# Finer pieces in the last turns of a streamed attention

## The reference

```python
def _L0_xattn_ref(query, ref, Wq, bq, Wk, bk, Wv, bv):
    Q = query @ Wq + bq
    K = ref @ Wk + bk
    V = ref @ Wv + bv
    scores = jnp.einsum('bqh,bkh->bqk', Q, K)
    attn = jax.nn.softmax(scores, axis=-1) * norm_fact
    return jnp.einsum('bqk,bkh->bqh', attn, V)

x = x + _L0_xattn_ref(_layernorm(x, axis=-1), ctx_1024, ...)
x = x + _L0_attn_ref(_layernorm(x, axis=-1), ...)
x = x + _L0_ffn_ref(_layernorm(x, axis=-1), ...)
```

## Time and profile before

| | us |
|---|---|
| median of three runs | 237.54 |
| the profiled execution | 237.44 |
| its span | 235.6 |
| TensorE matmul busy | 223.4 (95%) |
| VectorE busy | 138.4 (59%) |
| ScalarE busy | 134.2 (57%) |
| GpSimd busy | 106.0 (45%) |

### The profile page before, as it was taken

One profiled execution on the slowest core, in us unless ns is written; L12 is line 12 of the kernel. 1 busy time (PEld: TensorE's weight loads), 2 busy tenths in 40 slices (PEclk: granted clock), 3 DMA queues, 4 the chain that ended last, 5 costly groups with the idle time before them and its releaser, 6 DMA issues.

```text
span 235.6 us, 4164 instructions
## 1 busy us (share of the span) xinstructions
PE 223.4 (95%) x1537; PEld 190.3 (81%) x1537; DVE 138.4 (59%) x328; ACT 134.2 (57%) x251; POOL 106.0 (45%) x67
## 2 busy tenths in 40 slices
PE   7989999999999989779998999999999999999994
PEld 7747777777777767679987999874689999999993
DVE  3236555555555555625996777516144749977784
ACT  5145666665555557325795576636315858766570
POOL 1065566666666667330599940000000535555450
PEclk9999999999999999999999999999999999999999
DMA  6999999999999991699800000000000585970000
GB/s 207 370 425 415 417 417 420 415 420 418 419 418 418 405 424 78 239 432 420 334 3 3 0 3 0 1 3 0 0 0 3 181 335 200 406 307 3 3 0 22
DMA packets 8531, 52.92 MB, mean 225 GB/s; under 512 B 953, under 2 KB 1218, under 8 KB 6466
## 3 DMA queue, kind: packets, MB, share of 16 engines
q1 hardware_dynamic: 8514, 52.69, 55.8%
HBM read 52.56 MB, written 0.13 MB: 224 GB/s over the span
## 4 chain that ended last, share of the span: by engine, by line
PE 76%; DVE 9%; DMA 6%; ACT 4%; issue 2%; SPq 1%; POOL 1%; ACTq 0%; DVEq 0%; POOLq 0%
PE psum L440 34%; PE psum L508 14%; PE psum L744 8%; PE psum L435 7%; DMA late_sb<-in_ctx_T 6%; PE psum L639 3%; PE psum L626 2%; PE psum L431 2%; PE psum L668 2%; PE psum L695 1%; DVE work L1167 1%; DVE ring L1205 1%; DVE ring L1190 1%; DVE w_lo L1341 1%; POOL ring L387 1%
## 5 line engine op out<-in xcount | busy, mean ns | idle before, releaser
L368 POOL TENSOR_TENSOR ctx_lo<-ring,ctx_hi 128x1792 fp32r<-128x1792 f32 x13 | 52.5, 4035 | 39.8 <-ACT ctx_hi L808 39.8
L423 POOL TENSOR_TENSOR h_lo<-ring,h_hi 128x512 fp32r<-128x512 f32 x16 | 24.8, 1550 | 66.9 <-ACT h_hi L1000 61.0
L440 PE MATMUL psum<-late_sb,work 128*128 128x448 f32 x112 | 44.7, 542 | 1.2 <-DMA late_sb<-in_ctx_T 1.2
L440 PEld LDWEIGHTS psum<-late_sb,work 128*128 128x128 f32 x112 | 20.2, 190 | 18.1 <-issue 17.6
L815 ACT ACTIVATE probsT_hi<-psum 128x512 fp32r<-128x512 f32 (+1 forms) x28 | 13.7, 541 | 31.9 <-PE psum L435 31.9
L1060 DVE TENSOR_REDUCE smalls<-psum 128x1 f32<-128x896 f32 x14 | 15.3, 1092 | 23.1 <-PE psum L440 23.1
L440 PE MATMUL psum<-xT,late_sb 128*128 128x128 f32 x224 | 26.2, 276 | 0.1
L440 PEld LDWEIGHTS psum<-xT,late_sb 128*128 128x128 f32 x224 | 25.5, 192 | 0.3 <-DVE xT L1311 0.3
L808 ACT ACTIVATE ctx_hi<-ring 128x1792 fp32r<-128x1792 f32 x13 | 22.1, 1698 | 2.7 <-DMA ring<-in_ctx 2.7
L508 PE MATMUL psum<-ctx_hi,probsT_hi 128*128 128x256 f32 x98 | 20.6, 326 | 2.5 <-DVE probsT_lo L1084 2.5
L1084 DVE TENSOR_TENSOR probsT_lo<-psum,probsT_hi 128x512 fp32r<-128x512 f32 (+1 forms) x28 | 16.2, 620 | 7.4 <-ACT probsT_hi L815 7.4
(11 more groups left out here) (243 smaller groups left out, 420.3 us busy)
## 6 DMA issues: line engine op xcount, KB each, us to landing
late_sb<-in_ctx_T SPq DMA_DIRECT2D x14, 896.0 KB, 14.0
ring<-in_ctx SPq DMA_DIRECT2D x14, 896.0 KB, 12.8
late_sb<-in_late SPq DMA_DIRECT2D x10, 825.0 KB, 12.5
late_sb<-in_experts SPq DMA_DIRECT2D x8, 1024.0 KB, 6.3
late_slots<-in_experts SPq DMA_DIRECT2D x8, 1024.0 KB, 7.8
early_sb<-in_early SPq DMA_DIRECT2D x1, 512.0 KB, 3.7
early_sb<-in_early SPq DMA_DIRECT2D x1, 465.0 KB, 17.6
work<-in_levels SPq DMA_DIRECT2D x1, 416.0 KB, 20.0
```

The lines of the kernel that those rows point to most:

```text
L368: nc.gpsimd.tensor_tensor(ctxNv[1][:, r % 2], ring[:, r], ctxNv[0][:, r % 2], ALU.subtract).then_inc(s["ctx_lo"], 1)
L423: nc.gpsimd.tensor_tensor(hT[1][:, e % 2, at, :], h32[:, at, :], hT[0][:, e % 2, at, :], ALU.subtract).then_inc(s["h_lo_done"], 1)
L440: last = nc.tensor.matmul(o, lhs(c), rhs(c), start=(c == 0), stop=(c == n - 1))
```

## The change

Four things are done, the first in every turn and the others in the last turns.

1. `attend` takes the terms in the order high x high, high probabilities x low context, low probabilities x high context. It waits for the high probabilities at the start of each part and for the low ones at their first use. It can be called for a stretch of its terms (`first`, `end`) and with another division of the tiles (`cut`).
2. The last group's scores step `scores_ready` after each half. VectorE takes the maximum half by half, and ScalarE the exponential in two halves of 448 with two row sums, each with its own `exp_done`. SP waits for one more `scores_ready`.
3. The last group's probabilities are transposed as three tiles and four, the three ahead of the last three terms of the attend of group 12 and the four behind them. High and low parts and the last attend follow that division. The small exponential for `al` stands between the two high parts, the low context of three tiles ahead of the accumulation of group 12, and the row sums behind the low parts.
4. O is updated, transposed, copied and multiplied by halves of 128 columns, the transposes into banks 0 and 2.

```diff
-            def attend(g, r, last_group=False):
-                pe.wait_ge(s["acc_done"], g + 1)
-                pe.wait_ge(s["ctx_lo"], g + 1)
-                terms = [(t, a, b) for tiles in (range(4), range(4, GT)) for a, b in ((0, 0), (1, 0), (0, 1)) for t in tiles]
-                for i, (t, a, b) in enumerate(terms):
-                    if i == 0:
-                        pe.wait_ge(s["probsT_lo"], g * 2 + 1)
-                    if i == 4 * 3:
-                        pe.wait_ge(s["probsT_lo"], g * 2 + 2)
-                        if last_group:
+            def attend(g, r, first=0, end=3 * GT, cut=4, last_group=False):
+                if first == 0:
+                    pe.wait_ge(s["acc_done"], g + 1)
+                    pe.wait_ge(s["ctx_lo"], g + 1)
+                terms = [(t, a, b) for tiles in (range(cut), range(cut, GT)) for a, b in ((0, 0), (0, 1), (1, 0)) for t in tiles]
+                for i in range(first, end):
+                    t, a, b = terms[i]
+                    q = 0 if t < cut else 1
+                    if t == cut * q and (a, b) == (0, 0):
+                        pe.wait_ge(s["probsT_hi"], g * 2 + q + 1)
+                        if last_group and q == 1:
                             pe.wait_ge(s["last_lo"], 1)
+                    if t == cut * q and a == 1:
+                        pe.wait_ge(s["probsT_lo"], g * 2 + q + 1)
...
+            def last_transposes(q, tiles):
+                pe.wait_ge(s["exp_done"], NG + q)
+                pe.wait_ge(s["probsT_lo"], 2 * (NG - 1))
+                transposes([(bank[4 + q][:, k * P:(k + 1) * P], probs[:, t * P:(t + 1) * P]) for k, t in enumerate(tiles)], s["probs_transposed"])
...
-            scores(NG - 1, (NG - 1) % RING, 16 * ((NG - 1) // RING + 1))
-            attend(NG - 2, (NG - 2) % RING)
-            probs_transposes(NG - 1)
-            attend(NG - 1, (NG - 1) % RING, last_group=True)
+            scores(NG - 1, (NG - 1) % RING, 16 * ((NG - 1) // RING + 1), halves=True)
+            attend(NG - 2, (NG - 2) % RING, end=18)
+            last_transposes(0, range(0, 3))
+            attend(NG - 2, (NG - 2) % RING, first=18)
+            last_transposes(1, range(3, GT))
+            attend(NG - 1, (NG - 1) % RING, cut=3, last_group=True)
...
-            transposes([(half(bank[0], c), half(O, c)) for c in range(DC)], s["o_T"])
-            pe.wait_ge(s["o_copied"], 1)
-            wide(bank[1][:, 0:D], lambda c: half(OT, c), lambda c: wv[:, c, :]).then_inc(s["att_ready"], 1)
+            for c in range(DC):
+                pe.wait_ge(s["acc_done"], NG + 2 + c)
+                nc.tensor.transpose(half(bank[2 * c], 0), half(O, c), ident).then_inc(s["o_T"], 1)
+            for c in range(DC):
+                pe.wait_ge(s["o_copied"], c + 1)
+                last = nc.tensor.matmul(bank[1][:, 0:D], half(OT, c), wv[:, c, :], start=(c == 0), stop=(c == DC - 1))
+            last.then_inc(s["att_ready"], 1)
...
+            for hf in range(2):
+                nc.scalar.activation(probs[:, hf * HALF:(hf + 1) * HALF], bank[2 * b + hf][:, 0:HALF], ACT.Exp, bias=s_("nb", b, b + 1),
+                                     accum_out=s_("rowsum", hf, hf + 1)).then_inc(s["exp_done"], 1)
+            act.wait_ge(s["pv_done"], g)
+            for q, tiles in ((0, range(0, 3)), (1, range(3, GT))):
+                act.wait_ge(s["probs_transposed"], g * 2 + (q + 1))
+                nc.scalar.activation(probsT[0][:, tiles[0]:GT if q else 3, :], bank[4 + q][:, 0:len(tiles) * P].rearrange("p (t q) -> p t q", q=T),
+                                     ACT.Copy).then_inc(s["probsT_hi"], 1)
+                if q == 0:
+                    nc.scalar.activation(s_("al", b, b + 1), s_("M", (r + 1) % RING, (r + 1) % RING + 1), ACT.Exp, scale=-1.0,
+                                         bias=s_("M", r, r + 1)).then_inc(s["alpha_done"], 1)
+            for c in range(DC):
+                act.wait_ge(s["o_T"], c + 1)
+                nc.scalar.activation(half(OT, c), bank[2 * c][:, 0:P], ACT.Copy).then_inc(s["o_copied"], 1)
...
+            for hf in range(2):
+                dve.wait_ge(s["scores_ready"], NG + hf)
+                dve.wait_ge(s["mx_done"], 2 * g + 2 * hf)
+                V.tensor_reduce(s_("mx"), bank[2 * b + hf][:, 0:HALF], AX, ALU.max).then_inc(s["mx_done"], 1)
+                dve.wait_ge(s["mx_done"], 2 * g + 2 * hf + 1)
+                V.tensor_scalar(new, s_("mx"), s_("qb"), s_("M", r, r + 1) if hf == 0 else new, ALU.add, ALU.max).then_inc(s["mx_done"], 1)
+            dve.wait_ge(s["mx_done"], 2 * g + 4)
+            V.tensor_scalar(s_("nb", b, b + 1), new, -1.0, s_("qb"), ALU.mult, ALU.add).then_inc(s["max_ready"], 1)
             dve.wait_ge(s["dve_chain"], chain[0])
             V.tensor_tensor(ctxNv[1][:, g % 2, at], ring[:, g % RING, at], ctxNv[0][:, g % 2, at], ALU.subtract).then_inc(s["last_lo"], 1)
+            accumulate(g - 1, (g - 1) % 2)
...
+            for c in range(DC):
+                V.scalar_tensor_tensor(half(O, c), half(O, c), s_("al", b, b + 1), half(bank[6 + b], c), ALU.mult, ALU.add).then_inc(s["acc_done"], 1)
```

More of the change, by code:

```diff
@@ L333, in _ @@
                 part(i, "late2_in")
-            sp.wait_ge(s["scores_ready"], NG)
+            sp.wait_ge(s["scores_ready"], NG + 1)
             for j in range(SLOTS):
@@ L477, in _, with scores @@
             nc.tensor.matmul(bank[3][:, 0:D], sixteenth[:, :], bv_sb[:, :], start=True, stop=True).then_inc(s["bv_ready"], 1)
-            def scores(g, r, filled, first=False):
+            def scores(g, r, filled, first=False, halves=False):
                 if not first:
@@ L486, in scores @@
                                 lambda c: ringT[:, r, c, hf * HALF:(hf + 1) * HALF])
-                last.then_inc(s["scores_ready"], 1)
+                    if halves or hf == 1:
+                        last.then_inc(s["scores_ready"], 1)
             def probs_transposes(g, first=False):
@@ L495, in probs_transposes @@
                                s["probs_transposed"])
-            def attend(g, r, last_group=False):
-                pe.wait_ge(s["acc_done"], g + 1)
-                pe.wait_ge(s["ctx_lo"], g + 1)
-                terms = [(t, a, b) for tiles in (range(4), range(4, GT)) for a, b in ((0, 0), (1, 0), (0, 1)) for t in tiles]
-                for i, (t, a, b) in enumerate(terms):
-                    if i == 0:
-                        pe.wait_ge(s["probsT_lo"], g * 2 + 1)
-                    if i == 4 * 3:
-                        pe.wait_ge(s["probsT_lo"], g * 2 + 2)
-                        if last_group:
+            def attend(g, r, first=0, end=3 * GT, cut=4, last_group=False):
[9 more added lines that the diff above has]
+                        if last_group and q == 1:
                             pe.wait_ge(s["last_lo"], 1)
+                    if t == cut * q and a == 1:
+                        pe.wait_ge(s["probsT_lo"], g * 2 + q + 1)
                     last = nc.tensor.matmul(bank[6 + r % 2][:, 0:D], probsT[a][:, t, :], ctxNv[b][:, r % 2, t, :],
                                             start=(i == 0), stop=(i == len(terms) - 1))
-                last.then_inc(s["pv_done"], 1)
+                if end == 3 * GT:
+                    last.then_inc(s["pv_done"], 1)
+            def last_transposes(q, tiles):
+                pe.wait_ge(s["exp_done"], NG + q)
+                pe.wait_ge(s["probsT_lo"], 2 * (NG - 1))
+                transposes([(bank[4 + q][:, k * P:(k + 1) * P], probs[:, t * P:(t + 1) * P]) for k, t in enumerate(tiles)], s["probs_transposed"])
             pe.wait_ge(s["g_done"], 1)
@@ L529, in _ @@
             probs_transposes(NG - 2)
-            scores(NG - 1, (NG - 1) % RING, 16 * ((NG - 1) // RING + 1))
-            attend(NG - 2, (NG - 2) % RING)
-            probs_transposes(NG - 1)
-            attend(NG - 1, (NG - 1) % RING, last_group=True)
-            pe.wait_ge(s["tables_in"], 16)
-            pe.wait_ge(s["acc_done"], NG + 2)
-            transposes([(half(bank[0], c), half(O, c)) for c in range(DC)], s["o_T"])
-            pe.wait_ge(s["o_copied"], 1)
-            wide(bank[1][:, 0:D], lambda c: half(OT, c), lambda c: wv[:, c, :]).then_inc(s["att_ready"], 1)
+            scores(NG - 1, (NG - 1) % RING, 16 * ((NG - 1) // RING + 1), halves=True)
[4 more added lines that the diff above has]
+            attend(NG - 1, (NG - 1) % RING, cut=3, last_group=True)
+            pe.wait_ge(s["tables_in"], 16)
+            for c in range(DC):
[5 more added lines that the diff above has]
+            last.then_inc(s["att_ready"], 1)
             keep_warm(11)
@@ L836, in _ @@
             nc.scalar.activation(ctxNv[0][:, g % 2, at], ring[:, g % RING, at], ACT.Copy).then_inc(s["ctx_hi"], 1)
[L837 to L841, removed]
+            b, r = g % 2, g % RING
+            act.wait_ge(s["max_ready"], NG)
+            act.wait_ge(s["probs_transposed"], 2 * g)
+            act.wait_ge(s["acc_done"], NG)
```

(30 more changed lines are left out.)

## The result

| | before | changed |
|---|---|---|
| median of the runs, us | 237.62 (6 runs, 237.04 to 239.20) | 235.89 (6 runs, 235.10 to 236.64) |
| the profiled execution, us | 237.44 | 236.64 |
| its span, us | 235.6 | 234.8 |
| TensorE matmul busy, us | 223.4 | 226.2 |

The ratio is 0.9927, with a 95% interval of 0.9907 to 0.9947: 1.73 us less by the medians. A second set of six runs gave 235.51 us and a ratio of 0.9908 (0.9877 to 0.9940). The forecast was 235.3, or 2.17 us less.

A forecast was written before the change was run, and what follows sets the result against it. TensorE was taken to bound the steady turns, with 3.5 us idle in the last turns. 1.81 us up to the last attend plus 0.36 for O's halves is 2.17: 237.44 - 2.17 = 235.27, said 235.3; range 234.6 to 236.5.

The forecast's parts named there:

- Group 11: Its attend, needing low parts last, starts 0.72 us earlier; 0.35 is kept, as group 12's transposes wait for the exponential.
- The maximum in two halves: Last group: first half reduced before the last scores end, saving 0.49 us; bounds nothing and 0.55; exponential starts at 96.00.
- The exponential: Last group's, in two halves: first transpose loads 0.79 us after its start instead of 1.16, 0.37 less.
- TensorE's order: Transposes placed around group 12's last three terms: ScalarE's high part released at 97.78, last attend at 98.41 instead of 100.22.
- O: After the last attend, update, transposes and copy by halves save 0.36 us of 2.75 before x's update; bounds 0 and 0.6.
- Rest: Expert weights start 0.35 and 1.8 us earlier, no gain put down; everything after the attention stays in the same order.
- rival (d): A fixed event after the attention takes back up to all of the gain: 235.5 to 237.4 us; chance 0.07.
- Rival (b): 28 more waits on TensorE over all 14 attends cost 0.14 us each, 3.9 us: slower, 239.2 us; chance 0.06.
- Rival (a): Pieces cost what they save; only the order of terms gains, 1.07 us: 236.4 us; chance 0.15.
- Rival (c): ScalarE released by the transposes, or group 12's exponential no limit: up to 0.35 us more gain, 234.9 us; chance 0.12.

The follow-up runs named there:

- Experiment 8: Changed kernel with last group's VectorE context copy on ScalarE, ScalarE's last high parts released earlier, and VectorE copying three of group 12's context tiles: median 235.01 us, ratio 0.9885.
- experiment 2: Changed kernel with the last group's maximum and exponential each in one piece again: 236.01 us (one run).
- Experiments 4: Changed kernel with VectorE's copy of three context tiles moved between the two halves of the maximum, while GpSimd's subtraction runs: 237.99 us (one run).
- experiment 5: Changed kernel with VectorE's copy of three context tiles given to ScalarE: median 235.18 us, ratio 0.9896.
- experiment 10: Changed kernel with five more already satisfied waits in every attend, 70 in all on TensorE: median 235.61 us.
- experiment 1: Kernel before with only the new order of terms and the later wait for the low parts, in all attends: median 236.37 us, ratio 0.9931.
- experiment 6: Changed kernel with ScalarE's last high parts released after the 18th term of group 12's attend instead of its last: 235.50 us (one run).

## Why the prediction was right, and where it was off

Sign and mechanism were right, and the time lies in the range. Step by step, with the changed kernel's times less 0.97:

- *Group 11.* Its attend starts at 88.84 - 0.97 = 87.87 (87.88 forecast), released by ScalarE's high part. The transposes of group 12 load at 90.74 (90.74 forecast), held by the exponential. Experiment 8 takes this hold away and brings 0.34 of the 0.37 us that it kept back.
- *The maximum in two halves.* Here the prediction failed. It put the gain at 0.49 us, and its bounds named "nothing (the first half delayed)", but it took the time before the last scores to be enough for the first reduce without working out where VectorE's copy would then lie. Moved up by 0.38 us, the copy started 0.60 us before GpSimd's end instead of 0.22 and was held until then. GpSimd's end had not moved (10.25 us after the common point in both kernels), so the copy's end did not either: 10.66 before, 10.67 changed, which is 95.19. The first reduce started at 95.11, the second at 96.13 and not at 95.74, when the last scores were there (by experiment 2, 94.70 - 83.48 after the common point; in the changed profile itself, the transfer that SP issues on the same step starts at 95.73). The exponential started at 97.34 - 0.97 = 96.37, not 96.00. Against experiment 2, whose exponential starts 96.38 - 83.48 = 12.90 us after the common point, the changed kernel's 97.34 - 84.52 = 12.82 is all that the halved maximum brings: 0.08 and not 0.49. The saving of one reduce was sized well (1.09 less 0.62 = 0.47 us); it was the condition that failed, that the first one is done in time. Experiments 4, 5 and 8 show the copy and GpSimd as the cause.
- *The exponential.* From its start to the first transpose's load 98.12 - 97.34 = 0.78 us (0.79 forecast), as the 0.37 left over in experiment 2 also says (0.45 - 0.08).
- *TensorE's order.* ScalarE's high part was released by the end of group 12's attend, 99.06 - 98.40 = 0.66 us after the last three terms' first load, at 98.09. That is 0.31 after the 97.78 forecast: the 0.37 of the exponential, less some 0.05 since the three transposes took 98.40 - 98.12 = 0.28 and not 0.33. The last attend starts at 99.70 - 0.97 = 98.73, 0.32 after the forecast, and runs 2.78 us to O's update without a wait at its seventh term. The low context of three tiles took 1.02 us and not the 0.84 estimated, and was hidden all the same.
- *O.* 104.88 - 102.48 = 2.40 us, 0.35 less than before (0.36 forecast).
- *Rest.* Nothing came back later, so rival (d) is out. Rival (b) is out by the steady turns and experiment 10. Rival (a) is out too: without the pieces D is 21.08 (experiment 1) and with them 20.36. A pair of pieces does cost more than the whole, 2 x 0.62 against 1.09 us for the reduce, but half of each pair lay off the path, and what was lost was lost to a neighbour on another engine. Rival (c) did not happen: ScalarE was released by the attend's end, and the exponential of group 12 was the limit. Its price was about right, since experiment 6 takes the one away for 0.29 us and experiment 8 the other for 0.34.

So the sum was 2.17, and D shows 1.84. The 0.33 between them is in the main one term, mis-sized: 0.41 too much for the halved maximum. Against it stand 0.04 by which the last scores came earlier than forecast (95.74 - 0.97 = 94.77 against 94.81) and the 0.05 of the transposes; 0.01 was missing at O. That the first profile lay at 236.64 and not near 235.7 is the start's 0.97.

What the Trainium skill says of small tiles ("VectorE: DVE Perf Modes", on the TRN2 errata) is about operations that read SBUF, while the maximum, the exponential and the copies of O read PSUM here; it was a weak support for rival (a). On VectorE's copy of the context the Trainium skill has the matching rule, which I had not drawn on: "SBUF — State Buffer", section "SBUF: two separate sides", says that GpSimd and certain VectorE operations want the same pair of ports, and that whichever starts first has it for its whole instruction while the other waits. By that rule the copy ends a fixed time after GpSimd's instruction, and the rows agree: 0.41 to 0.42 us in each case, and the copy took up to 2.27 - 0.55 = 1.7 us longer.

## What to carry to other kernels

When a step moves earlier, lay every neighbour on every engine at its new time, also those that were hidden: a small copy was moved up by 0.38 us with the rest, but its end hung on another engine's long instruction that had not moved, and that cost 0.39 us of the gain. Where an operand is split into a high and a low part, order the products so that the low part is needed last: here that alone brought 1.12 of the 1.84 us, and the cutting into pieces 0.72 as it stood and 1.11 once the copy was out of its way (experiment 5). Measure a change at the end of one stage by a distance between two points of the trace, since the whole time also holds the noise of the start.

## What was not expected of the hardware

**VectorE's copy and GpSimd exclude each other.** A copy of 128 x 768 from fp32 to fp32r within SBUF took 0.55 us with GpSimd idle, 1.02 where it began 0.60 before GpSimd's end, and 2.27 where it began 1.85 before it, the last two ending 0.41 to 0.42 behind. The lengths fit one account: about 0.14 us of the copy's 0.55 pass before it needs GpSimd to be done, and the rest follows GpSimd's end (0.63 us where it began 0.22 before it). It works the other way too. GpSimd's own next instruction (128 x 1024) took 2.38 to 2.40 us undisturbed and 2.70 to 2.72 where the copy still ran at its start. VectorE's subtraction of the low context, with two inputs in SBUF, seems to be held in the same way, though no experiment was made on it. It took 0.95 us in the kernel before, behind GpSimd's end. In experiment 5 it ends at 97.14, 0.81 us after GpSimd's 93.93 + 2.40 = 96.33, and in the changed kernel 0.82 us after GpSimd's end (98.25 against 94.72 + 2.71 = 97.43); it cost nothing there. The half reduces from PSUM, 0.61 to 0.62 us in all runs, were not held.

**TensorE's first matmuls have two paces.** The eight matmuls of the query projection, in the changed kernel's profile and then in that of the kernel before:

```profile
6.78 2.08 PE L463 MATMUL psum<-xT,early_sb 128*128 128x128 f32 x8
```

```profile
5.93 1.16 PE L463 MATMUL psum<-xT,early_sb 128*128 128x128 f32 x8
```

2.08 us against 1.16, at a granted clock of 1.00 in both views. Three of the twelve profiles (the changed kernel, experiments 4 and 10) show the slow form, and in these the common point lies at 84.52 to 84.58 us; in the nine others (1.16 us, and 1.24 in experiment 8) it lies at 82.42 to 83.82. The pace changes at a moment that differs between executions. Four 128 x 64 matmuls on the constant tile took 0.69 us at the slow pace and 0.45 at the fast one: in the kernel before they took 0.45 from 4.36 us on, in experiment 8 0.69 at 4.70 and 0.45 at 7.95, and in the changed kernel's profile still 0.69 at 8.79. Not all of it reaches the common point: in the kernel before TensorE then stood idle for 0.96 us for the transposed context's transfer, in the changed kernel's profile it did not. The repeat of the changed kernel, the same program, shows the fast form. What makes the difference was not found.
